# Both ends of the expert stage: weights signalled by kind, additions ahead of low parts, a down product between two halves of the last gate-up

## The chip, the cores and the metric

The kernel runs on one core of a Trainium2 chip. The metric is the time of one execution on the device in microseconds (us), lower is better. Engines are named as in the profile: PE is TensorE, PEld its weight loads, DVE is VectorE, ACT is ScalarE, POOL is GpSimd, SP is SyncE (it only issues DMAs here).

## What is computed

`x` is 8 sequences of 112 tokens of width 512, that is 896 tokens.

```python
x = x + attention(layernorm(x), ctx, Wq, Wkv_expand, Wout)     # 16 heads of 32, causal mask
h = layernorm(x)
scores = softmax(h @ gate_weight.T); topk_w, topk_idx = top_k(scores, 2)     # 8 experts
gu = einsum('th,efh->tef', h, gate_up_weights)                 # 512 -> 2 x 352 for each expert
y = einsum('tef,te,ehf->th', silu(gu[..., :F]) * gu[..., F:], combine, down_weights)
sgu = h @ shared_gate_up.T                                     # shared expert, 512 -> 2 x 704
y = y + (silu(sgu[:, :Fs]) * sgu[:, Fs:]) @ shared_down.T
out = x + y
```

## The kernel before

Each engine has an instruction stream of its own, written out by hand, and waits for the others by named semaphores. Products are made in fp32r from split operands: a value is held as a high part (rounded, written by a copy on ACT or POOL) and a low part (value less high part, written by DVE), and three products hi x lo, lo x hi, hi x hi stand for one.

Attention comes first, then the shared expert, six blocks of its inner width (`shared_gu`, `shared_down`; NJ = 6, ND = 5), whose results `add_shared` on DVE adds into `xres`. Meanwhile the tokens are sorted by expert and written by an indirect DMA into 21 tiles (NT) of 128 rows in DRAM; each tile belongs to one expert, whose number is read from `eid` by a `value_load` on every engine that addresses weights.

The expert stage runs over the 21 tiles. For tile i:

- SP loads it (`load_x`, semaphore `xin`); PE transposes it (`t_x`) into bank `S[2]`; ACT and DVE split it (`xs_hi`, `xs_lo`).
- ACT and DVE split the expert's gate-up weights in four chunks of 128 rows (`gu_hi`, `gu_lo`, buffer `gu_parts`), each as soon as the previous tile's product of the same chunk has been made.
- PE makes `gate_up(i)`: four chunks x three split passes x two banks (gate columns into `S[0]`, up columns into `S[1]`), 24 products. Each chunk counts one on `eg`.
- ACT takes silu of the gate bank, DVE multiplies it with the up bank (`expert_act`, semaphore `eact`).
- PE makes `down(i - 1)` (six split products and one plain one for the last 96 rows), then `t_act(i)`, the transposes of the activations, which ACT and DVE split again (`put_actT`, `aT_lo`).
- Two 128 x 512 high parts of the down weights are written by ACT (`dn_hi`) and POOL (`dn_hi1`), one low part for both by DVE (`dn_lo`).
- ACT copies y of tile i - 1, scaled by the routing weight, into `y_sb` (`put_y`, semaphore `ey`); POOL adds it into `out` with an indirect DMA (L505) after it has waited for the landing of the one before it (`yst`), since two rows of one token may not be added at once.

On PE tiles 2 to 19 are a loop (`Fori`); tiles 0, 1 and 20 are written out. The last tile is done without splits: `put_last_actT` and a DVE copy give `act_last`, and `last_down` makes its product in two column parts, which `put_last_y` copies out. `fill_with_transposes` makes transposes that nobody reads.

At the beginning of the stage PE has still to make the last shared product (`shared_down(ND - 1, ...)`): four banks of t = 0, then `t_x(0)`, then two of the three banks of t = 1, then `gate_up(0)`. The banks of t = 1 are those of t = 0, so each waits for an addition (`sres`). All expert weights are signalled on one semaphore, `we`, except the last three down weights, on `we_late`, whose loads are issued when the shared gate-up weights have been used. ACT waits for `we` before it splits the first gate-up chunk:

```python
act.wait_ge(s["pos"], 3)
act.wait_ge(s["we"], 16 * (3 * E - 2 * n_late))
act.wait_ge(s["sg"], NBLK * NJ)
e = expert(0)
for c in range(C):
    gu_hi(e, 0, c, first=True)
```

Here E = 8, C = 4, n_early = 1 and n_late = 3: eight gate-up loads, and two DMAs for each of the five early down weights.

Of the kernel before, what the change touches and what calls it, by code (L numbers as in the profile page):

```python
# [42 lines left out]
def build(nc, x, ctxT, wqT, wkvT, woT, gateT, guT, dnT, sguT, sdnT, out):  # L43
    NB, SQ, H = x.shape
    L = ctxT.shape[0]
    C = H // P
# [3 lines left out]
    E = guT.shape[0]  # L50
    F = dnT.shape[1]
# [9 lines left out]
    NX = T // P  # L61
# [162 lines left out]
    def ring_parts(b):  # L224
# [6 lines left out]

    names = (

        "x0 xt1 xt2 xrest wq0 wq1 wq2 wq3 wkeys wvals wo wgate ctx0 ctx1 wsg0 wsg1 wsd0 wsd1 wsd2 we we_late "

        "const zt sel zero wgpad sumg idf "

# [15 lines left out]
    with nc.Block() as block:  # L253
# [3 lines left out]
        def _(sp):  # L257
# [42 lines left out]
            def load_gu(e, sem):  # L300
                sp.dma_start(w_gu[:, e * GU:(e + 1) * GU], guT[e].rearrange("p c f -> p (c f)")).then_inc(sem, 16)

            def load_dn(e, sem):
                k2 = F // P * P
                at = w_dn[:, e * DN:(e + 1) * DN].rearrange("p (k d) -> p k d", d=H)
                sp.dma_start(at[:, 0:k2 // P, :],
                             dnT[e, 0:k2, :].rearrange("(k p) d -> p k d", p=P)).then_inc(sem, 16)
                sp.dma_start(at[0:F - k2, k2 // P, :], dnT[e, k2:F, :]).then_inc(sem, 16)
# [17 lines left out]
                sp.dma_start(xs_in[:, 0:H], xs_dram[bass.ds(i * P, P), 0:H]).then_inc(s["xin"], 16)  # L326

            for e in range(0, 2):
                load_gu(e, s["we"])
            next_sd(2)  # L330
            next_sg(2)
            for e in range(2, 5):
                load_gu(e, s["we"])
            next_sg(3)
            next_sd(3)
            for e in range(5, E):
                load_gu(e, s["we"])
            for e in range(n_early):
                load_dn(e, s["we"])
            next_sd(5)  # L340
            next_sg(4)
            next_sd(4)
# [4 lines left out]
            sp.wait_ge(s["ysum0"], 16)  # L347
            load_x(0)
            for e in range(n_early, E - n_late):
                load_dn(e, s["we"])  # L350
            sp.dma_start(dest[:, :, :], xs_dram[:, H:H + 2].bitcast(U32).rearrange("(n p) o -> p n o", p=P),
                         allow_slow_non_contiguous=True).then_inc(s["dest"], 16)
            sp.wait_ge(s["sg"], NBLK * NJ)
            for e in range(E - n_late, E):
                load_dn(e, s["we_late"])


            sp.wait_ge(s["Tx"], 1)
# [20 lines left out]
        def _(pool):  # L379
# [102 lines left out]
            scatter(1, "scat2")  # L482

            pool.wait_ge(s["pos"], 3)
            pool.wait_ge(s["we"], 16 * (3 * E - 2 * n_late))
            pool.wait_ge(s["we_late"], 16 * 2 * n_late)
            pool.wait_ge(s["sdn"], NX * ND)

            def dn_hi1(i):
                e = pool.value_load(eid[0:1, i:i + 1], min_val=0, max_val=E - 1)  # L490
                if i >= 1:
                    pool.wait_ge(s["edn_split"], i)
                pool.tensor_copy(dn2[0][:, 1, :], w_dn[:, bass.ds(e * DN + H, H)]).then_inc(s["dn_hi1"], 1)  # L493

# [16 lines left out]
        def _(pe):  # L511
# [316 lines left out]
            def gate_up(i, chunks=range(C)):  # L828

                pe.wait_ge(s["xs_hi"], i + 1)  # L830
                pe.wait_ge(s["xs_lo"], i + 1)
                for c in chunks:
                    pe.wait_ge(s["gu_hi"], C * i + c + 1)
                    pe.wait_ge(s["gu_lo"], C * i + c + 1)
                    for n, (x_, w_) in enumerate(((0, 1), (0, 0), (1, 0))):
                        for dst, f0 in ((S[0], 0), (S[1], F)):
                            ins = pe.matmul(dst[:, 0:F], xsT[x_][:, c, :], gu2[w_][:, c, f0:f0 + F],  # L837
                                            start=c == 0 and n == 0, stop=c == C - 1 and n == 2)
                    ins.then_inc(s["eg"], 1)

            def expert(i):
                return pe.value_load(eid[0:1, bass.ds(i, 1)], min_val=0, max_val=E - 1)

            def down(i, e):
                pe.wait_ge(s["aT_hi"], i + 1)
                pe.wait_ge(s["aT_lo"], i + 1)
                pe.wait_ge(s["dn_hi"], i + 1)
                pe.wait_ge(s["dn_hi1"], i + 1)
                pe.wait_ge(s["dn_lo"], i + 1)
                product(A[:, :], [(both(actT_split, every, k, every), both(dn2, every, k, every)) for k in range(2)],  # L850
                        stop=False).then_inc(s["edn_split"], 1)
                pe.wait_ge(s["aT"], i + 1)
                w = FK[2][1]
                pe.matmul(A[:, :], actT_plain[0:w, :], w_dn[0:w, bass.ds(e * DN + 2 * H, H)],  # L854
                          start=False, stop=True).then_inc(s["edn"], 1)
# [17 lines left out]
            def t_act(i):  # L873
                pe.wait_ge(s["eact"], i + 1)
                for k, (f0, w) in enumerate(FK):
                    ins = pe.transpose((S[3] if k < 2 else B)[0:w, k * P:(k + 1) * P], act_e[:, f0:f0 + w], ident[:, :])  # L876
                ins.then_inc(s["Ta"], 1)
# [6 lines left out]
            gate_up(1)  # L884
            t_x(2)
            pe.wait_ge(s["pos"], 3)
            pe.wait_ge(s["we"], 16 * (3 * E - 2 * n_late))
            pe.wait_ge(s["we_late"], 16 * 2 * n_late)
            down(0, expert(0))
            t_act(1)  # L890
            with pe.Fori(2, NT - 1) as i:
# [4 lines left out]
                down(i - 1, e)  # L896
                t_act(i)
            e_last = [expert(i) for i in (NT - 2, NT - 1)]
            gate_up(NT - 1)
            pe.wait_ge(s["ey"], NT - 2)  # L900
            down(NT - 2, e_last[0])
            t_act(NT - 1)
            fill_with_transposes(S[2], 5)
            pe.wait_ge(s["sres"], NX * ND)
            last_down(NT - 1, e_last[1])

# [2 lines left out]
        def _(act):  # L909
# [195 lines left out]
                hi(dn2[0][:, 0, :], w_dn[:, bass.ds(e * DN, H)], "dn_hi")  # L1105

            def silu(i):
                act.wait_ge(s["eg"], C * (i + 1))
                act.activation(silu_e[:, :], S[0][:, 0:F], ACT.Silu).then_inc(s["esil"], 1)  # L1109

            def put_y(i):
# [23 lines left out]
                act.activation(actT_plain[0:w, :], B[0:w, 2 * P:3 * P], ACT.Copy).then_inc(s["aT"], 1)  # L1135

            act.wait_ge(s["pos"], 3)
            act.wait_ge(s["we"], 16 * (3 * E - 2 * n_late))

            act.wait_ge(s["sg"], NBLK * NJ)  # L1140
            e = expert(0)
# [3 lines left out]
            for i in range(NT):  # L1145
                if i + 1 < NT:
                    e_next = expert(i + 1)
                    for c in range(C - 1):
                        gu_hi(e_next, i + 1, c)
                if i == NT - 1:  # L1150
                    silu(i)
                    put_last_actT(i)
                    put_y(i - 1)
                    break
                silu(i)
                xs_hi(i + 1)
                gu_hi(e_next, i + 1, C - 1)
                if i == 0:
                    act.wait_ge(s["sdn"], NX * ND)
                    act.wait_ge(s["we_late"], 16 * 2 * n_late)  # L1160
                    act.wait_ge(s["dest"], 16)
                dn_hi(e, i)
                if i >= 1:
                    put_y(i - 1)
                put_actT(i)
                e = e_next
# [4 lines left out]
        def _(dve):  # L1171
# [324 lines left out]

            def expert_act(i):
                dve.wait_ge(s["esil"], i + 1)
                dve.tensor_tensor(act_e[:, :], S[1][:, 0:F], silu_e[:, :], ALU.mult).then_inc(s["eact"], 1)  # L1499

            def aT_lo(i):
# [3 lines left out]
            for c in range(C):  # L1505
                if c == 2:
                    xs_lo(0)
                gu_lo(e, 0, c)
                add_shared(ND - 1, 0, c, c + 1)
            add_shared(ND - 1, 1, 0, 2)  # L1510
            for i in range(NT):
                if i + 1 < NT:
# [51 lines left out]
```

## Time and profile before

| | |
|---|---|
| median of 3 runs | 351.46 us (351.35 to 352.0) |
| profiled execution | 353.07 us, its span 351.3 us |
| PE busy | 332.9 us (95% of the span) |
| DVE, ACT, POOL busy | 271.6, 230.0, 118.5 us |
| mean granted clock of PE | 0.992 of 2.4 GHz |

Times in the rows are us from the start of the span; a duration is that of one instruction or of a merged group (x24: 24 of them). "[0.51 <-DVE xres]" is idle time of the engine just before, and who ended it. A matmul's own duration overlaps with that of the next; in the chain only the part that nothing else covers is counted.

### The profile page before, as it was taken

Reading aid. Unit: us, or ns where it says so; the run is one execution under the profiler, and the core shown is the slowest. Engines: PE = TensorE matmul, PEld = TensorE weight load, DVE = VectorE, ACT = ScalarE, POOL = GpSimd, SP = SyncE. Lnnn points to the kernel's source line nnn. Section 1 sums busy time; section 2 is a strip of 40 time slices with the busy share of each in tenths; the row PEclk is TensorE's granted clock in tenths of the full one; section 3 lists DMA queues with packets and bytes.
Section 4 is the critical chain, followed back from the end, with each engine's and each line's share of the span. In section 5 each row is a group of like instructions: output and inputs, shape, how many; then the busy total and the mean of one; then the engine's idle time right before and its main releaser. Section 6 shows DMA issues by size and latency. Waiting matters only on the chain.

```text
span 351.3 us, 7091 instructions
## 1 busy us (share of the span) xinstructions
PE 332.9 (95%) x2281; PEld 280.5 (80%) x2282; DVE 271.6 (77%) x464; ACT 230.0 (65%) x586; POOL 118.5 (34%) x136
## 2 busy tenths in 40 slices
PE   6999989999999999999999999999999999999980
PEld 6898877777776797988897878898889889988860
DVE  4798978999946258835586998999899899989900
ACT  3577899999973233213235578888888888888720
POOL 3332753555541000256200033343244234324411
PEclk9999999999999999999999999999999999999996
DMA  7999100000003799993599735434443543444233
GB/s 253 368 349 380 64 3 2 3 2 2 2 2 108 284 331 387 400 355 129 169 292 246 261 101 86 93 60 72 82 88 60 82 92 67 67 82 91 30 41 49
DMA packets 29051, 49.47 MB, mean 141 GB/s; under 512 B 7136, under 2 KB 12256, under 8 KB 28000
## 3 DMA queue, kind: packets, MB, share of 16 engines
q1 hardware_dynamic: 24880, 39.91, 35.0%
q0 software_dynamic: 4144, 9.23, 15.0%
q8 instruction: 13, 0.21, 0.3%
q14 instruction: 14, 0.11, 0.1%
HBM read 32.22 MB, written 16.92 MB: 140 GB/s over the span
## 4 chain that ended last, share of the span: by engine, by line
PE 54%; ACT 14%; DVE 10%; DMA 9%; issue 5%; POOL 4%; SPq 1%; POOLq 1%; ACTq 0%; DVEq 0%
PE bank L837 22%; PE bank L524 19%; ACT prob L956 8%; PE bank L854 5%; POOL xs_dram L474 4%; DMA xs_dram<-x2n,slot_i 3%; DMA w_dn<-dnT 3%; PE bank L708 2%; PE bank L876 2%; ACT probT L911 2%; PE bank L737 1%; DMA out<-y_sb,dest 1%; DVE xres L1391 1%; DMA w_sg<-sguT 1%; DMA ctx<-ctxT 1%
## 5 line engine op out<-in xcount | busy, mean ns | idle before, releaser
L1186 DVE TENSOR_TENSOR gu_parts<-w_gu,gu_parts 128x704 fp32r<-128x704 f32 x84 | 78.9, 972 | 1.7 <-ACT gu_parts L911 1.6
L911 ACT ACTIVATE gu_parts<-w_gu 128x704 fp32r x84 | 66.2, 794 | 18.4 <-PE bank L837 17.2
L837 PE MATMUL bank<-gu_parts,xsT_hi 128*128 128x352 f32 x336 | 69.5, 328 | 0.8 <-DVE xsT_lo L1186 0.8
L837 PEld LDWEIGHTS bank<-gu_parts,xsT_hi 128*128 128x128 f32 x336 | 55.6, 189 | 1.6 <-issue 1.2
L493 POOL CAST dn_hi<-w_dn 128x512 fp32r x20 | 19.7, 984 | 101.0 <-PE bank L524 69.0
L505 POOL DMA_INDIRECT out<-y_sb,dest x21 | 33.3, 1585 | 22.9 <-ACT y_sb L1116 17.2
L837 PE MATMUL bank<-gu_parts,xsT_lo 128*128 128x352 f32 x168 | 40.9, 325 | 0.0
L524 PE MATMUL bank<-x2T_hi,w_sg_lo 128*128 128x512 f32 (+1 forms) x88 | 32.6, 371 | 0.3
L524 PE MATMUL bank<-x2T_hi,w_sg_hi 128*128 128x512 f32 (+1 forms) x88 | 32.0, 363 | 0.0
L524 PE MATMUL bank<-x2T_lo,w_sg_hi 128*128 128x512 f32 (+1 forms) x88 | 31.9, 363 | 0.0
L837 PEld LDWEIGHTS bank<-gu_parts,xsT_lo 128*128 128x128 f32 x168 | 29.3, 189 | 0.0
L911 ACT ACTIVATE act_s_hi<-act_s 128x512 fp32r<-128x512 f32 (+1 forms) x10 | 5.8, 578 | 32.4 <-DVE act_s L1371 20.2
L474 POOL DMA_INDIRECT xs_dram<-x2n,slot_i x14 | 14.3, 1019 | 37.1 <-DVE eid L1471 33.1
L1186 DVE TENSOR_TENSOR dn_lo<-w_dn,dn_hi 128x1024 fp32r<-128x1024 f32 x20 | 24.6, 1228 | 0.8 <-POOL dn_hi L493 0.8
L956 ACT ACTIVATE prob<-score,negmax 112x112 f32<-112x112 f32 x64 | 24.1, 411 | 0.0
L956 ACT ACTIVATE prob<-bank,negmax 112x112 f32<-112x112 f32 x64 | 21.8, 363 | 1.9 <-DVE negmax L1231 1.9
L1391 DVE TENSOR_TENSOR xres<-xres,bank 128x512 f32<-128x512 f32 x35 | 22.0, 677 | 0.0
L854 PE MATMUL bank<-w_dn,actT_plain 96*128 x40 | 20.5, 592 | 0.0
L524 PEld LDWEIGHTS bank<-x2T_hi,w_sg_lo 128*128 128x128 f32 x88 | 16.5, 188 | 4.9 <-issue 2.5
L1499 DVE TENSOR_TENSOR act_e<-bank,silu_e 128x352 f32<-128x352 f32 x21 | 11.0, 523 | 11.8 <-ACT silu_e L1109 11.8
L911 ACT ACTIVATE probT<-bank 112x448 f32<-112x448 f32 x32 | 16.6, 554 | 3.9 <-PE bank L708 3.9
L404 POOL TENSOR_TENSOR prob<-prob,rrow 112x448 f32<-112x448 f32 x16 | 14.7, 931 | 11.7 <-DVE rrow L1235 11.7
(196 smaller groups left out, 804.9 us busy)
## 6 DMA issues: line engine op xcount, KB each, us to landing
w_gu<-guT SPq DMA_DIRECT2D x8, 1408.0 KB, 9.7
xs_dram<-no_row SPq DMA_DIRECT2D x1, 5460.0 KB, 19.2
xs_in<-xs_dram SPq DMA_DIRECT2D x21, 256.0 KB, 2.6
w_dn<-dnT SPq DMA_DIRECT2D x8, 512.0 KB, 6.2
w_sg<-sguT SPq DMA_DIRECT2D x10, 256.0 KB, 5.6
w_dn<-dnT SPq DMA_DIRECT2D x8, 192.0 KB, 6.7
w_sd<-sdnT SPq DMA_DIRECT2D x5, 256.0 KB, 4.8
out<-xres SPq DMA_DIRECT2D x1, 1280.0 KB, 5.4
```

Source lines behind the costliest of these rows:

```text
L404: pool.tensor_tensor(prob[r][:, :, :], prob[r][:, :, :], rrow[:, r, :].unsqueeze(2).to_broadcast([SQ, C, SQ]), ALU.mult)\
L474: pool.indirect_dma_start(out=xs_dram[:, :], out_offset=bass.IndirectOffsetOnAxis(ap=slot_i[:, k, n:n + 1], axis=0), in_=x2n[:, n, :], in_ ...
L493: pool.tensor_copy(dn2[0][:, 1, :], w_dn[:, bass.ds(e * DN + H, H)]).then_inc(s["dn_hi1"], 1)
L505: pool.indirect_dma_start(out=out[:, :], out_offset=bass.IndirectOffsetOnAxis(ap=dest[:, i, 0:1], axis=0), in_=y_sb[i % 2][:, :], in_offse ...
L524: ins = pe.matmul(dst, a, b, start=start and n == 0, stop=stop and n == len(passes) - 1)
L837: ins = pe.matmul(dst[:, 0:F], xsT[x_][:, c, :], gu2[w_][:, c, f0:f0 + F], start=c == 0 and n == 0, stop=c == C - 1 and n == 2)
L854: pe.matmul(A[:, :], actT_plain[0:w, :], w_dn[0:w, bass.ds(e * DN + 2 * H, H)], start=False, stop=True).then_inc(s["edn"], 1)
L911: act.activation(dst, src, ACT.Copy).then_inc(s[sem], 1)
L956: ins = act.activation(prob[r][:, c, :], src, ACT.Exp, bias=negmax[:, r, c:c + 1], accum_out=rowsum[:, r, c:c + 1])
L1186: dve.tensor_tensor(lo_, src, hi_.bitcast(F32), ALU.subtract).then_inc(s[sem], 1)
L1391: dve.tensor_tensor(xres[:, n, :], xres[:, n, :], (B, CC, D, A)[i][:, :], ALU.add)\
L1499: dve.tensor_tensor(act_e[:, :], S[1][:, 0:F], silu_e[:, :], ALU.mult).then_inc(s["eact"], 1)
```

## The change

1. The semaphore `we` becomes `wegu` (eight gate-up loads) and `wedn` (early down weights); `we_late` is now `wedn_late`. ACT waits for `wegu` ahead of its first chunk and for `wedn` ahead of its first `dn_hi`. POOL makes its first `value_load` ahead of its waits for down weights and shared products.
2. DVE makes each of the first four `add_shared` ahead of `gu_lo` of the same chunk, not behind it.
3. The last gate-up is made in two halves: chunks 0 and 1 in the usual order, then `down(19)`, then chunks 2 and 3, all gate columns first (`last_gate_then_up`). Silu of tile 20 waits for the gate columns only, the product on DVE for both.
4. ACT copies y of tile 19 ahead of silu(20). Fillers are eight ahead of `t_act(20)` (none before) and four behind it (five before).

```diff
-            for e in range(n_early):
-                load_dn(e, s["we"])
+            for e in range(n_early):
+                load_dn(e, s["wedn"])
...
             pool.wait_ge(s["pos"], 3)
-            pool.wait_ge(s["we"], 16 * (3 * E - 2 * n_late))
-            pool.wait_ge(s["we_late"], 16 * 2 * n_late)
-            pool.wait_ge(s["sdn"], NX * ND)

             def dn_hi1(i):
                 e = pool.value_load(eid[0:1, i:i + 1], min_val=0, max_val=E - 1)
-                if i >= 1:
+                if i == 0:
+                    pool.wait_ge(s["wedn"], 16 * 2 * (E - n_late))
+                    pool.wait_ge(s["wedn_late"], 16 * 2 * n_late)
+                    pool.wait_ge(s["sdn"], NX * ND)
+                else:
                     pool.wait_ge(s["edn_split"], i)
...
+            def last_gate_then_up(chunks):
+                i = NT - 1
+                for dst, f0 in ((S[0], 0), (S[1], F)):
+                    for c in chunks:
+                        pe.wait_ge(s["gu_hi"], C * i + c + 1)
+                        pe.wait_ge(s["gu_lo"], C * i + c + 1)
+                        for n, (x_, w_) in enumerate(((0, 1), (0, 0), (1, 0))):
+                            ins = pe.matmul(dst[:, 0:F], xsT[x_][:, c, :], gu2[w_][:, c, f0:f0 + F],
+                                            start=False, stop=c == C - 1 and n == 2)
+                    ins.then_inc(s["eg"], 1)
...
-            gate_up(NT - 1)
+            gate_up(NT - 1, range(C // 2))
             pe.wait_ge(s["ey"], NT - 2)
             down(NT - 2, e_last[0])
+            last_gate_then_up(range(C // 2, C))
+            fill_with_transposes(S[2], 8)
             t_act(NT - 1)
-            fill_with_transposes(S[2], 5)
+            fill_with_transposes(S[2], 4)
...
-                act.wait_ge(s["eg"], C * (i + 1))
+                act.wait_ge(s["eg"], C * (i + 1) - (i == NT - 1))
...
-            act.wait_ge(s["we"], 16 * (3 * E - 2 * n_late))
+            act.wait_ge(s["wegu"], 16 * E)
...
                 if i == NT - 1:
+                    put_y(i - 1)
                     silu(i)
                     put_last_actT(i)
-                    put_y(i - 1)
                     break
...
                 if i == 0:
                     act.wait_ge(s["sdn"], NX * ND)
-                    act.wait_ge(s["we_late"], 16 * 2 * n_late)
+                    act.wait_ge(s["wedn"], 16 * 2 * (E - n_late))
+                    act.wait_ge(s["wedn_late"], 16 * 2 * n_late)
...
                 dve.wait_ge(s["esil"], i + 1)
+                if i == NT - 1:
+                    dve.wait_ge(s["eg"], C * NT)
...
+                add_shared(ND - 1, 0, c, c + 1)
                 gu_lo(e, 0, c)
-                add_shared(ND - 1, 0, c, c + 1)
```

## Rows read from the trace of the kernel before

**Rows 1.** The page: granted clock of PE in 40 slices of 8.8 us, tenths.

```profile
PEclk9999999999999999999999999999999999999996
```

**Rows 2.** The chain, a gate-up in the loop: start, us, what.

```profile
317.70 3.89 PE bank L837 x24
```

**Rows 3.** The chain at the beginning of the stage: the load ACT waits for.

```profile
178.32 9.49 DMA w_dn<-dnT
```

**Rows 4.** Timeline of PE there: start, us, instruction, idle time ahead and its releaser.

```profile
187.03 0.40 PE L524 MATMUL bank<-w_sd_hi,act_s_lo 128*128 128x512 f32 x1
...
188.19 0.39 PE L524 MATMUL bank<-w_sd_hi,act_s_lo 128*128 128x512 f32 x1
...
190.47 0.46 PE L737 MATMUL bank<-ident_f,xs_in 128*128 128x128 f32 x4
191.44 0.47 PE L524 MATMUL bank<-w_sd_hi,act_s_lo 128*128 128x512 f32 x1 [0.51 <-DVE xres L1391]
...
194.00 0.81 PE L837 MATMUL bank<-gu_parts,xsT_hi 128*128 128x352 f32 x4
```

**Rows 5.** Timeline of ACT and DVE there.

```profile
186.97 0.53 ACT L911 ACTIVATE act_p<-silu_s 64x384 fp32r<-64x384 f32 x1 [0.74 <-DVE silu_s L1371]
...
187.53 0.55 DVE L1380 TENSOR_TENSOR act_p<-silu_s,act_p 64x384 fp32r<-64x384 f32 x1 [0.59 <-ACT act_p L911]
...
188.74 2.83 ACT L911 ACTIVATE gu_parts<-w_gu 128x704 fp32r x4 [1.25 <-DMA w_dn<-dnT]
...
189.68 0.89 DVE L1186 TENSOR_TENSOR gu_parts<-w_gu,gu_parts 128x704 fp32r<-128x704 f32 x1 [1.60 <-ACT gu_parts L911]
```

**Rows 6.** Timeline of POOL, DVE and PE where PE enters its loop.

```profile
201.59 0.61 POOL L493 CAST dn_hi<-w_dn 128x512 fp32r x1 [32.00 <-issue]
...
202.35 1.23 DVE L1186 TENSOR_TENSOR dn_lo<-w_dn,dn_hi 128x1024 fp32r<-128x1024 f32 x1 [0.83 <-POOL dn_hi L493]
...
206.59 0.55 PE L876 MATMUL bank<-ident,act_e 128*128 128x128 f32 x3
207.91 0.89 PE L837 MATMUL bank<-gu_parts,xsT_hi 128*128 128x352 f32 x4 [0.77 <-DVE xsT_lo L1186]
```

**Rows 7.** The chain at the end.

```profile
331.38 4.03 PE bank L837 x24
...
337.64 0.34 PE bank L876 x3
...
338.29 0.69 ACT y_sb L1116
...
339.24 4.93 DMA out<-y_sb,dest
```

**Rows 8.** Timeline of all engines at the end.

```profile
332.06 1.56 POOL L505 DMA_INDIRECT out<-y_sb,dest  x1 [0.64 <-ACT y_sb L1116]
...
333.23 0.41 DVE L1186 TENSOR_TENSOR actT_split_lo<-bank,actT_split_hi 128x256 fp32r<-128x256 f32 x1
...
335.94 0.52 DVE L1499 TENSOR_TENSOR act_e<-bank,silu_e 128x352 f32<-128x352 f32 x1 [2.30 <-ACT silu_e L1109]
...
338.56 2.87 PE L865 MATMUL bank<-w_dn,act_last 96*128 x12
...
340.86 0.98 ACT L1123 ACTIVATE y_sb<-bank,dest 128x384 f32<-128x384 f32 x2 [1.89 <-PE bank L865]
344.92 1.54 POOL L505 DMA_INDIRECT out<-y_sb,dest  x1 [4.13 <-DMA out<-y_sb,dest]
```

**Rows 9.** Tile w_gu from 130 us: the last loads of gate-up weights, issue times.

```profile
L301 SPq DMA_DIRECT2D w_gu<-guT x3: 431/432/433, 136.1 to 137.0; - x3
```

**Rows 10.** DMA issues from 190 to 192 us: KB, us from issue to landing.

```profile
xs_in<-xs_dram SPq DMA_DIRECT2D x1, 256.0 KB, 5.8
```

**Rows 11.** Timeline of DVE in the loop, pairs of low parts.

```profile
326.73 1.70 DVE L1186 TENSOR_TENSOR gu_parts<-w_gu,gu_parts 128x704 fp32r<-128x704 f32 x2
...
330.06 2.10 DVE L1186 TENSOR_TENSOR gu_parts<-w_gu,gu_parts 128x704 fp32r<-128x704 f32 x2
```

More of the change, by code:

```diff
@@ L232, in build @@
     names = (
-        "x0 xt1 xt2 xrest wq0 wq1 wq2 wq3 wkeys wvals wo wgate ctx0 ctx1 wsg0 wsg1 wsd0 wsd1 wsd2 we we_late "
+        "x0 xt1 xt2 xrest wq0 wq1 wq2 wq3 wkeys wvals wo wgate ctx0 ctx1 wsg0 wsg1 wsd0 wsd1 wsd2 wegu wedn wedn_late "
         "const zt sel zero wgpad sumg idf "
@@ L328, in _ @@
             for e in range(0, 2):
-                load_gu(e, s["we"])
+                load_gu(e, s["wegu"])
             next_sd(2)
@@ L332, in _ @@
             for e in range(2, 5):
-                load_gu(e, s["we"])
+                load_gu(e, s["wegu"])
             next_sg(3)
@@ L336, in _ @@
             for e in range(5, E):
-                load_gu(e, s["we"])
+                load_gu(e, s["wegu"])
             for e in range(n_early):
-                load_dn(e, s["we"])
+                load_dn(e, s["wedn"])
             next_sd(5)
@@ L349, in _ @@
             for e in range(n_early, E - n_late):
-                load_dn(e, s["we"])
+                load_dn(e, s["wedn"])
             sp.dma_start(dest[:, :, :], xs_dram[:, H:H + 2].bitcast(U32).rearrange("(n p) o -> p n o", p=P),
@@ L354, in _ @@
             for e in range(E - n_late, E):
-                load_dn(e, s["we_late"])
+                load_dn(e, s["wedn_late"])
             sp.wait_ge(s["Tx"], 1)
@@ L886, in _ @@
             pe.wait_ge(s["pos"], 3)
-            pe.wait_ge(s["we"], 16 * (3 * E - 2 * n_late))
-            pe.wait_ge(s["we_late"], 16 * 2 * n_late)
+            pe.wait_ge(s["wedn"], 16 * 2 * (E - n_late))
+            pe.wait_ge(s["wedn_late"], 16 * 2 * n_late)
             down(0, expert(0))
```

## Prediction

> **What bounds the kernel now.** I read the page first: TensorE is busy 95% of the span and its granted clock is high in every slice but the last [rows 1], so time can only be won where TensorE waits or where the end hangs on something else. Then the chain that ended last, over the expert stage. From tile 3 to tile 19 it is TensorE alone: the gate-ups of tiles 18 and 20 start at 317.70 and 331.38, two tiles of 6.84 us [rows 2, 7], the same for every tile between. Reordering can win nothing there, and the change touches nothing there. At both ends the chain leaves TensorE, and those are the places to price.
>
> At the beginning the chain runs over a down weight that lands at 187.82 [rows 3], ScalarE's first gu_parts at 188.74 after 1.25 idle, VectorE's low part at 189.68 after 1.60 idle [rows 5], an addition of the shared result behind it, and TensorE, which waits 0.51 for that addition till 191.44 [rows 4]. All this time the result to be added was there: the next bank's products start at 187.03 [rows 4], so the first bank was full near 187.2.
>
> A second place is the loop's entry [rows 6]: VectorE stands 0.83 idle for GpSimd's first cast at 201.59, then works without a gap of note up to xsT_lo of tile 2, and 0.77 after that TensorE starts gate-up(2), at 207.91. Its activation transposes had ended at 206.59 + 0.55 = 207.14.
>
> At the end [rows 7, 8] gate-up(20) ends at 331.38 + 4.03 = 335.41 and down(19) at 337.64, but y of tile 19 is copied out only at 338.29 to 338.98, since ScalarE does silu(20) and act_last first. Its scatter goes at 339.24 (0.27 after the copy), takes 4.93, lands at 344.17, and 0.75 later, at 344.92, the last scatter starts. The last y had been ready since 340.86 + 0.98 = 341.84. So the end hangs on the scatter of tile 19, and the last y has 344.92 - 341.84 - 0.27 = 2.8 us of slack.
>
> **The start, edit by edit.** ScalarE's wait for the gate-up weights only: the last of those loads was issued at 137.0 [rows 9], fifty us ahead, so it is passed at once. ScalarE's sequencer is then free when the act_p copy has gone out at 186.97 [rows 5]. From the landing to the first chunk it needed 188.74 - 187.82 = 0.92, value load and dispatch. The first chunk therefore starts near 187.9, 0.85 earlier; the four (2.83) end at 190.7, when the transposes of x (190.47 and about 0.3) have just ended. xsT_hi follows at once, and xsT_lo is ready near 192.1.
>
> Additions in front of the low parts are the same instructions, swapped. VectorE's own value load can follow 187.53 [rows 5], so the first addition goes at 187.53 + 0.92 = 188.45 and ends at 189.1; the second, behind a low part of 0.8, ends at 190.6. TensorE wants them at 190.76 and 191.92, five products of one tile taking 187.03 to 188.19 = 1.16 [rows 4]. Both waits are gone: gate-up(0) starts at 190.76 + 2 x 1.16 = 193.08, not 194.00. Its own needs are there (xsT_lo 192.1, two low parts 191.4); chunks 2 and 3, now behind additions, come at 193.6 and 195.0 and are wanted a half and three quarters through, at 195.0 and 196.0. Gain 0.92.
>
> What is late next is x of tile 1: issued when the transposes of tile 0 are done, about 190.96, it took 5.8 [rows 10] and lands at 196.8, and that does not move. TensorE will want it after gate-up(0), at 193.08 + 3.89 = 196.97. It just fits. The down weights' waits now stand on ScalarE ahead of its first dn_hi, eleven us after the first chunk, with y and the activation split behind; even loads as slow as the 9.49 of [rows 3], issued by 189.7, would be in by 199.2, about when it comes there. I cost it at nothing.
>
> GpSimd's waits behind the value load: the last shared product ended near 199.5 and the cast came at 201.59, 2.1 later, of which I take the value load to be most. With it done beforehand the cast comes near 198.7 and VectorE's 0.83 goes. But the cast then lies beside a low part: a pair of low parts that shares its time with a cast takes 2.10, a pair without 1.70 [rows 11]. I charge 0.40. VectorE's chain to xsT_lo(2) moves by 0.9 + 0.83 - 0.4 = 1.33 and gate-up(2) with it, to 206.58. TensorE itself would be ready at 207.14 - 0.92 = 206.22. So the bounds of the start are 0.9 (the cast brings nothing) and 1.7. I take **1.3**.
>
> The Trainium skill (SBUF — State Buffer, Who interferes with whom) says that a VectorE instruction with two SBUF inputs and a GpSimd one that reads SBUF exclude each other, the later being blocked for the whole of the other. By it the cast could cost VectorE its full 0.61, and the time would be 0.2 above my forecast. The trace agrees that they contend, with 0.40.
>
> **The end, edit by edit** (times as in the trace of before, the start's gain not taken off). Gate-up(20) starts at 331.38; half of it is done at 333.4. Down(19) now comes here and needs actT_split_lo, which VectorE ends at 333.64 [rows 8]. This is the new wait: TensorE goes on at 333.75. Down takes 2.23 as before (335.41 to 337.64) and 0.1 to restart, and ends at 336.1. y(19) is now first on ScalarE, 336.12 to 336.81, and its scatter goes at 337.08, if scatter 18 is in; that went at 332.06, and with 19's 4.93 and the 0.75 it would allow 337.74. It was 339.24.
>
> Behind put_y on ScalarE stand silu(20) and act_last. Of the second half, gate columns end at 336.1 + 0.97 = 337.07, when ScalarE is free, up columns at 338.05. Silu and product took 335.41 to 336.46 [rows 8], hidden under down(19); now silu is hidden by the up columns and the product's 0.52 is exposed, till 338.6, where VectorE's added wait for both halves holds nothing else up. The eight fillers lie over it. Three transposes take 0.34 [rows 7], 0.11 each, so eight end at 338.93, 0.3 after the data: the fill, not the data, sets it. Then t_act until 339.27. From its end to last_down it was 338.56 - 337.98 = 0.58 with five fillers, so with four 0.47: last_down at 339.75. From there to the last y it is 341.84 - 338.56 = 3.28, giving 343.05, and its scatter can go at 343.32.
>
> Scatter 19 lands at 337.08 + 4.93 = 342.0 and allows the last at 342.75. The last y is the later, so the last scatter starts at 343.3 instead of 344.92; from there to the end nothing changes. Gain **1.6**. Bounds: 2.2 if only the scatters count; 0.8 if an issue stall as long as TensorE's 0.77 of [rows 6] stands in the rewritten tail.
>
> The Trainium skill (DMA: Bandwidth & Descriptors, Anatomy of one DMA — SWDGE (gpsimd) path) gives about 2.0 us plus bytes / 436e3. An estimate by it for 256 KB is 2.6 us; by that the old end would have hung on scatter 19 only until 342.6, and a last y at 343.05 would lose some 0.7 at this end. The trace shows 4.93 for this scatter and decides against it.
>
> **The sum.** 1.3 + 1.6 = 2.9 us. The profiled execution took 353.07 (span 351.3, 1.8 around it), so 350.2 for one like it. The median of the runs, 351.46, lies 1.6 below the profiled one; with the same difference, 348.5.
>
> **Rivals.**
> - Start lost: x of tile 1 comes late, or VectorE's chain does not shorten. For it stands that x has 0.2 us to spare, against it 2.4 us of idle time on VectorE. 0.3 + 1.6: 349.6.
> - End half lost: a stall of 0.8 in the tail. For it: the half product waits on VectorE's last instruction and new code is fetched; against: leaving the loop cost 0.14 (4.03 for 3.89). 1.3 + 0.8: 349.4.
> - More: TensorE enters the loop when it is ready, and the last y does not hold up. 1.7 + 2.2: 347.6.
> - The change doesn't do what it says: the value loads, not the waits, took the time, and another landing replaces 19's. 351.4.
> - Slower: the 0.35 gap ahead of down(19), with little work around it, lets the clock fall from 2.4 to 1.2 GHz. Left from there are 2.3 + 1.9 + 0.9 + 0.3 + 2.9 = 8.3 us of TensorE, doubled; 8.3 - 2.9 = 5.4 lost: 356.9. It decides as soon as 2.9 us of work is doubled. Against it: the gap of 0.77 at 207 left the clock's slice at 9, and only the last slice, which holds no product, reads 6 [rows 1].
>
> **How the numbers follow.** Forecast 0.53 (its own range 347.9 to 349.2), start lost 0.13, end half lost 0.12, more 0.10, nothing 0.05, slower 0.07. The first four, 0.88, lie in 347.4 to 350.1, which takes in the bounds of both ends. A measurement of this kernel can tell about 0.2%, 0.7 us: faster 0.88, same 0.05, slower 0.07.
>
> **What would show it.** Start: ScalarE's first gu_parts near 187.9, no wait of TensorE at 191, gate-up(0) at 193.1, the cast near 198.7, gate-up(2) near 206.6. End, counted from the start of gate-up(20): down(19) at +2.4 (was +4.0), its scatter at +5.7 (was +7.9), the last at +11.9 (was +13.5), released by y and not by a landing. I am wrong if the last scatter is still released by a landing beyond +13, if x of tile 1 shows as a wait, or if the granted clock drops ahead of the last product.

## The result and the profile after

Seven runs of each kernel on one chip: 351.39 us before (350.69 to 352.25), 349.79 us after (349.05 to 351.91). The ratio is 0.9949, 95% interval 0.9925 to 0.9973: 1.8 us faster, between 0.9 and 2.6; the two medians lie 1.6 apart. The forecast was 348.5, 2.9 us faster, in a range of 347.4 to 350.1. The time lies in that range, near its slow end and outside the 347.9 to 349.2 that I had given the forecast itself. The gain came out at some two thirds of what I had summed up, and 2.9 lies just outside the interval.

The profiled execution after took 349.05 us with a span of 347.3, 4.0 less than the one before. That is more than the change gives. The first product with `act_p` (L767 before, L768 after), which closes the first bank of the last shared product and which no edit reaches, starts at 186.49 before and at 185.37 after, so 1.1 us is not of the change. I therefore count from this product, called R below, up to the loop, and from the start of gate-up(20) at the end. These are timeline starts; the chain of [rows 7] has gate-up(20) at 331.38, since it counts only what nothing else covers. Timeline of TensorE in the kernel before: R, gate-up(1), gate-up(20) and down(19):

```profile
186.49 0.47 PE L767 MATMUL bank<-w_sd_lo,act_p 128*128 128x512 f32 x1
...
200.02 0.88 PE L837 MATMUL bank<-gu_parts,xsT_hi 128*128 128x352 f32 x4
...
331.30 0.88 PE L837 MATMUL bank<-gu_parts,xsT_hi 128*128 128x352 f32 x4
...
335.25 0.40 PE L524 MATMUL bank<-dn_hi,actT_split_lo 128*128 128x512 f32 x1
```

The start, TensorE's timeline in the kernel after (start, us, instruction, idle time ahead), against [rows 4, 6]:

```profile
185.37 0.47 PE L768 MATMUL bank<-w_sd_lo,act_p 128*128 128x512 f32 x1
...
189.35 0.46 PE L738 MATMUL bank<-ident_f,xs_in 128*128 128x128 f32 x4
189.65 0.46 PE L525 MATMUL bank<-w_sd_hi,act_s_lo 128*128 128x512 f32 x1
...
191.99 0.80 PE L838 MATMUL bank<-gu_parts,xsT_hi 128*128 128x352 f32 x4
...
197.90 0.89 PE L838 MATMUL bank<-gu_parts,xsT_hi 128*128 128x352 f32 x4
...
205.26 0.88 PE L838 MATMUL bank<-gu_parts,xsT_hi 128*128 128x352 f32 x4 [0.30 <-issue]
```

The wait of 0.51 behind the transposes of x is gone. Gate-up(0), (1), (2) start at 6.62, 12.53 and 19.89 from R; before it was 7.51, 13.53 and 21.42. ScalarE, GpSimd and VectorE there, against [rows 5, 6]:

```profile
185.85 0.53 ACT L925 ACTIVATE act_p<-silu_s 64x384 fp32r<-64x384 f32 x1 [0.74 <-DVE silu_s L1386]
186.78 2.84 ACT L925 ACTIVATE gu_parts<-w_gu 128x704 fp32r x4 [0.41 <-issue]
...
197.72 2.10 DVE L1201 TENSOR_TENSOR gu_parts<-w_gu,gu_parts 128x704 fp32r<-128x704 f32 x2
197.75 1.32 POOL L494 CAST dn_hi<-w_dn 128x512 fp32r x1 [29.29 <-PE bank L769]
199.74 1.21 DVE L1201 TENSOR_TENSOR dn_lo<-w_dn,dn_hi 128x1024 fp32r<-128x1024 f32 x1
```

The first chunk comes 0.93 after the copy of act_p goes out, with no landing in its way, and dn_lo follows without a wait. The cast now lies beside a pair of low parts, which takes 2.10, as in the loop [rows 11].

The end, all engines, against [rows 7, 8]:

```profile
328.71 0.88 PE L838 MATMUL bank<-gu_parts,xsT_hi 128*128 128x352 f32 x4
...
331.22 0.47 PE L525 MATMUL bank<-dn_hi,actT_split_lo 128*128 128x512 f32 x1 [0.34 <-issue]
...
333.74 0.69 ACT L1130 ACTIVATE y_sb<-bank,dest 128x512 f32<-128x512 f32 x1 [4.17 <-PE bank L866]
334.70 0.46 ACT L1123 ACTIVATE silu_e<-bank 128x352 f32<-128x352 f32 x1 [0.27 <-PE bank L849]
334.85 1.55 POOL L506 DMA_INDIRECT out<-y_sb,dest  x1 [3.86 <-ACT y_sb L1130]
335.45 1.03 PE L883 MATMUL bank<-ident 128*128 128x128 f32 x8
335.72 0.52 DVE L1516 TENSOR_TENSOR act_e<-bank,silu_e 128x352 f32<-128x352 f32 x1 [4.71 <-PE bank L849]
336.32 0.52 PE L888 MATMUL bank<-ident,act_e 128*128 128x128 f32 x3
...
337.44 2.87 PE L877 MATMUL bank<-w_dn,act_last 96*128 x12 [0.15 <-issue]
339.74 0.98 ACT L1137 ACTIVATE y_sb<-bank,dest 128x384 f32<-128x384 f32 x2 [2.47 <-PE bank L877]
340.99 1.54 POOL L506 DMA_INDIRECT out<-y_sb,dest  x1 [4.59 <-ACT y_sb L1137]
```

What released the last scatter was a landing before, [4.13 <-DMA out<-y_sb,dest] in [rows 8]; now it is y. From gate-up(20)'s start: down(19) at 2.51 (3.95 before), its scatter at 6.14 (7.94), last y ready at 12.01 (10.54), last scatter at 12.28 (13.62). The last y is 1.5 us later and the last scatter 1.3 us earlier. In these two traces the start won 21.42 - 19.89 = 1.53 and the end 1.34; with the 1.12 ahead of R that is all of the 4.0 between the spans.

### The profile page after: what moved, and what is told of

Read it like the earlier page. It is cut to its first block, busy times and chain, and to the rows that moved or that the text cites. A ratio compares the mean times of both kernels' runs of the same rounds, so it can differ in the third digit from the quotient of the medians.

```text
span 347.3 us, 7108 instructions
## 1 busy us (share of the span) xinstructions
PE 333.8 (96%) x2288; PEld 282.7 (81%) x2289; DVE 271.9 (78%) x464; ACT 230.3 (66%) x586; POOL 120.1 (35%) x136
## 4 chain that ended last, share of the span: by engine, by line
PE 74%; ACT 13%; DVE 6%; issue 3%; DMA 2%; POOLq 1%; POOL 1%; SPq 0%; DVEq 0%
PE bank L525 35%; PE bank L838 23%; ACT prob L970 8%; PE bank L866 5%; PE bank L888 2%; PE bank L709 2%; PE bank L738 2%; ACT probT L925 2%; PE bank L609 2%; DMA out<-y_sb,dest 1%; DVE xnT_lo L1201 1%; DMA w_sg<-sguT 1%; DVE prob L1254 1%; PE bank L517 1%; PE bank L580 1%
## 5 line engine op out<-in xcount | busy, mean ns | idle before, releaser
L838 PE MATMUL bank<-gu_parts,xsT_hi 128*128 128x352 f32 x328 | 67.9, 328 | 0.3 <-issue 0.3
L838 PEld LDWEIGHTS bank<-gu_parts,xsT_hi 128*128 128x128 f32 x328 | 54.2, 189 | 1.2 <-issue 1.0
L494 POOL CAST dn_hi<-w_dn 128x512 fp32r x20 | 20.7, 1035 | 97.8 <-PE bank L525 68.5
L838 PE MATMUL bank<-gu_parts,xsT_lo 128*128 128x352 f32 x164 | 39.9, 324 | 0.0
L866 PE MATMUL bank<-w_dn,actT_plain 96*128 x40 | 20.5, 591 | 0.0
```

## The experiments

Twelve runs, ten of altered kernels and one each of the two kernels once more. The traces of all are summed up first, in us: gate-up(0) to (2) and ScalarE's first chunk from R; TensorE's wait for x of tile 1; last y ready and last scatter from gate-up(20)'s start. "Landing" means that ScalarE's first chunk waited for a down weight to land, "free" that it did not.

| kernel | ACT chunk | gu(0) | gu(1) | gu(2) | x wait | last y | last scatter |
|---|---|---|---|---|---|---|---|
| before | 2.25, landing | 7.51 | 13.53 | 21.42 | 0 | 10.54 | 13.62 |
| before_again | 2.83, landing | 8.10 | 14.11 | 22.04 | 0 | 10.54 | 13.33 |
| y_first | 3.31, landing | 8.57 | 14.59 | 22.27 | 0 | 13.90 | 14.17 |
| end_only | 1.46, free | 6.73 | 12.75 | 20.75 | 0 | 12.05 | 12.32 |
| start_only | 1.41, free | 6.62 | 13.51 | 20.96 | 0.93 | 10.54 | 13.38 |
| after | 1.41, free | 6.62 | 12.53 | 19.89 | 0 | 12.01 | 12.28 |
| after_again | 1.41, free | 6.62 | 13.74 | 21.19 | 1.17 | 12.01 | 12.28 |
| fill0 | 1.42, free | 6.62 | 12.53 | 19.89 | 0 | 12.02 | 12.29 |
| gate_first_undone | 1.41, free | 6.62 | 12.53 | 19.88 | 0 | 12.45 | 12.72 |
| x_ahead_of_one | 1.41, free | 6.61 | 12.52 | 20.00 | 0 | 12.00 | 12.27 |
| dest_behind_x | 1.41, free | 6.62 | 12.87 | 23.99 | 0.29 | 12.03 | 12.31 |
| pool_undone | 1.41, free | 6.63 | 12.53 | 20.44 | 0 | 12.04 | 12.31 |
| adds_undone | 1.41, free | 6.70 | 13.23 | 20.62 | 0.50 | 12.01 | 12.28 |
| actwait_undone | 2.79, landing | 6.94 | 14.71 | 22.10 | 1.73 | 12.02 | 12.30 |

The four top ones have the old start, the others the new one, whole, less one part, or with its loads in another order.

**after_again**: the changed kernel, unaltered.

> The changed kernel, unaltered, once more. Theory A (both ends won 1.5 and 1.3 us, as the first trace of it shows, and the rest is chance): the stretch between the start of the last shared down product of half t = 0 and gate-up(2), 20.83 us now and 22.36 before, and the stretch from gate-up(20) to the last scatter, 12.24 now and 13.54 before, come out the same within 0.2 us; the ratio to before is about 0.992 (2.8 us). Rival B (something outside the two ends gives part of it back in most executions): the two stretches repeat, but the ratio stays at 0.995, and the part ahead of the expert stage is longer than in the trace of before.

349.9 us to 352.27 of the kernel before on the same chip, ratio 0.9944 (0.992 to 0.9967). The first result repeats; the interval rules out neither 0.992 at its edge nor 0.995. The end repeats to 0.01 us. The start does not: gate-up(0) is where it was, but then TensorE waits.

```profile
197.42 0.53 PE L738 MATMUL bank<-ident_f,xs_in 128*128 128x128 f32 x4 [1.17 <-DMA xs_in<-xs_dram]
```

x of tile 1 landed 1.2 us too late, and gate-up(2) came at 21.19, close to the 21.42 of the kernel before. This is the first rival of the prediction, in some executions and not in others. Theory A's "within 0.2" fell for the start. Rival B has the ratio right, but not its cause: what was given back lies in the start itself.

**start_only** and **end_only**: one half of the change each.

```diff
# start_only: the changed kernel with the end of the kernel before
-            gate_up(NT - 1, range(C // 2))
+            gate_up(NT - 1)
...
-            last_gate_then_up(range(C // 2, C))
-            fill_with_transposes(S[2], 8)
...
# end_only: the changed kernel with the three edits of the start undone
+            act.wait_ge(s["wedn"], 16 * 2 * (E - n_late))
...
-                add_shared(ND - 1, 0, c, c + 1)
                 gu_lo(e, 0, c)
+                add_shared(ND - 1, 0, c, c + 1)
```

> Only parts 1 and 2 of the change (signals by kind, POOL's value load ahead of its waits, additions in front); the end as before. Theory A: from the last shared down product of t = 0 to gate-up(2) it takes 20.8 us instead of 22.4; gate-up(20) to the last scatter stays at 13.5; ratio 0.9956 (1.5 us). Rival (the start's gain is taken back later by the loop): the beginning of the loop comes earlier but gate-up(20) does not, ratio 1.0.

> Only parts 3 and 4 of the change (down(19) between the halves, gate columns first, y of tile 19 first, fillers 8 and 4); the start as before. Theory A: gate-up(20) to the last scatter takes 12.2 us instead of 13.5, ratio 0.9963 (1.3 us). Rival (scatters set the end whatever the order, and the last landing only slides): the last scatter is released by a landing again and the stretch takes over 13.0, ratio 0.999 to 1.

Ratios 0.9981 (0.9958 to 1.0005) and 0.9989 (0.9965 to 1.0014). Theory A had said 0.9956 and 0.9963, and each lies just outside its interval; 1.0, no change, lies inside both. So the runs show neither half by itself, and added up they give 1.1 us where both together gave 1.8 and 2.0. Medians on that chip: 352.27 before, 351.67, 351.28, and 349.9 with both. Times of single executions spread over 3 us and more, so the traces must tell. In end_only's trace the last scatter is at 12.32, released by y: the end does its work alone, and the rival of a sliding landing falls. In start_only gate-up(0) is at 6.62, but x of tile 1 was 0.93 late, so gate-up(2) was 20.96 and not 19.9.

**fill0**: no transposes ahead of the last `t_act`.

```diff
-            fill_with_transposes(S[2], 8)
```

> The changed kernel without the eight fillers ahead of the last activation transposes. Theory A (the fillers, not the data, set the start of these transposes, as worked out beforehand): in the trace of after the data are there at 336.24 and the fillers end at about 336.49, so the transposes come 0.2 us earlier and the last scatter 0.2 earlier, at 12.05 from gate-up(20). Rival (they hold the clock up): the granted clock falls ahead of the last product and last_down, 2.87 us, takes more than 3.5 us.

Ratio 0.9959 (0.9935 to 0.9982). Last scatter at 12.29: nothing won, and last_down still takes 2.87. Both theories fell. act_e is ready 7.53 after gate-up(20)'s start in the kernel after (336.24 - 328.71) and 7.55 here (336.28 - 328.73), and the transposes start at 7.61 or 7.60 in either: the eight fillers end just as the data comes, and so cost nothing.

**x_ahead_of_one** and **dest_behind_x**: two ways to have x of tile 1 sooner.

```diff
# x_ahead_of_one
-            for e in range(E - n_late, E):
+            for e in range(E - n_late, E - 1):
                 load_dn(e, s["wedn_late"])
...
             load_x(1)
+            load_dn(E - 1, s["wedn_late"])
```

> The changed kernel with the load of the last down weight (704 KB) issued behind the load of x of tile 1 and not ahead of it. Theory A (in some executions x of tile 1 lands after gate-up(0), behind the late down weights, and holds TensorE): no wait of TensorE for xs_in; from the first act_p product (the reference point, first L768 row of the stage) to gate-up(1) it takes 12.5 us and to gate-up(2) 19.9, as in the first trace of the changed kernel and unlike the 13.7 and 21.2 of its second; median 0.5 to 1 us under that of the changed kernel. Rival B (x was late by chance of that one execution and costs little in the mean): median as the changed kernel. Rival C (the displaced weight is now what is late): a wait of ScalarE or GpSimd for a landing of w_dn ahead of dn_hi, reference point to gate-up(2) over 20.5.

> The changed kernel with the table of destinations (21 KB in elements of 8 bytes, over 2,600 packets) loaded behind x of tile 1. Theory A: the table occupies the DMA engines for about 2 us, in which 5 to 20 GB/s move, so x of tile 1 lands up to 2 us earlier and TensorE does not wait for it; gate-up(1) at 12.5 and gate-up(2) at 19.9 from the reference point. Rival C: the table itself is now late, ScalarE waits for it ahead of its first dn_hi and gate-up(2) comes at over 20.5. Rival B: nothing measurable.

x_ahead_of_one: 349.86 us to 352.14 before, ratio 0.9939 (0.9915 to 0.9964). Its trace has no wait for x although it was in the worse position: its stage loads (x of tile 0, the down weights right behind) began 11.4 us ahead of R, as in after_again (11.3), and not 13.3 as in the first trace of the changed kernel. That fits theory A, but in time it can't be told from the changed kernel (0.9949, 0.9944), so B's "costs little in the mean" isn't ruled out either. dest_behind_x has 0.9927 (0.99 to 0.9954); its profiled execution took 354.04 us and is not in that ratio. In it x of tile 1 is late by 0.29 and x of tile 2 by 1.34, so the wait moved one tile on. Most of what makes gate-up(2) so late there, 23.99, comes behind that wait: TensorE idles once more, for 0.99, and then its granted clock falls to 0.50, its level of 1.2 GHz, and the products of down(0) follow each other at 0.43 us and not 0.23. TensorE's timeline, and a window with busy times and, as the number behind POOL's, the granted clock:

```profile
204.42 0.53 PE L738 MATMUL bank<-ident_f,xs_in 128*128 128x128 f32 x4 [1.34 <-DMA xs_in<-xs_dram]
205.95 0.77 PE L525 MATMUL bank<-dn_hi,actT_split_lo 128*128 128x512 f32 x1 [0.99 <-issue]
206.51 0.63 PE L525 MATMUL bank<-dn_lo,actT_split_hi 128*128 128x512 f32 x1
```

```profile
206.00:208.00 2.00, 2.00 (x5) 1.61 (x6) 1.92 (x3) 0.27 (x1) 0.00 (x0) 0.50 0.47 131
```

How the table of destinations holds the DMA engines is seen in after_again; the view of DMA from 185 to 189 us, first line busy tenths in 40 slices, second GB/s:

```profile
DMA  9999999999999999688754433320359992249924
GB/s 369 328 309 288 189 92 156 115 137 97 98 97 77 96 93 51 9 9 8 6 6 5 5 5 3 2 3 21 102 123 246 307 184 82 82 143 184 123 82 143
DMA packets 2935, 0.45 MB, mean 112 GB/s; under 512 B 2727, under 2 KB 2727, under 8 KB 2935
```

In 4 us 2,727 packets under 512 bytes, and the engines busy while they move under 160 GB/s and then under 10. That the loads of down weights, and x of tile 1 behind them, are late by this is not shown: with the table moved behind it, x of tile 1 still took 6.4 us from issue to landing, against 5.8 in [rows 10]. Theory A of dest_behind_x fell in that trace; gate-up(2) passes rival C's 20.5, but by the wait for x and by the clock, since ScalarE's first dn_hi waits for nothing.

**pool_undone** and **adds_undone**: one edit of the start taken back.

```diff
# pool_undone
+            pool.wait_ge(s["wedn"], 16 * 2 * (E - n_late))
+            pool.wait_ge(s["wedn_late"], 16 * 2 * n_late)
+            pool.wait_ge(s["sdn"], NX * ND)
...
-                if i == 0:
...
+                if i >= 1:
```

> The changed kernel with GpSimd's waits ahead of its first value load again. Theory A (the value load, about 2 us, was on VectorE's way to the loop): the first cast comes 2.1 us after the last shared product and not at 0.4, VectorE idles for it, and gate-up(1) to gate-up(2) takes 7.9 us instead of 7.4. Rival (TensorE's own entry into the loop sets it): 7.4 as with it.

> The changed kernel with the four additions behind the low parts again. Theory A (once ScalarE is early, the order is worth little, since the first addition only has to be done when TensorE comes to the bank again): gate-up(0) at 6.7 us from the reference point instead of 6.6. Rival, as I worked it out beforehand (both edits together win 0.9 and the first addition at 190.6 was what held TensorE): with low parts first, the addition ends behind TensorE's arrival and gate-up(0) comes at 7.0 or later.

pool_undone, 0.9978 (0.9958 to 0.9998): gate-up(1) to (2) takes 7.91, where it is 7.36 with the edit and 7.89 before. VectorE waits for the cast again:

```profile
200.34 0.62 POOL L493 CAST dn_hi<-w_dn 128x512 fp32r x1 [31.43 <-issue]
...
201.09 1.22 DVE L1200 TENSOR_TENSOR dn_lo<-w_dn,dn_hi 128x1024 fp32r<-128x1024 f32 x1 [0.85 <-POOL dn_hi L493]
```

Theory A holds: the value load ahead of its waits is worth 0.55 us at the loop's entry. adds_undone, 0.9962 (0.9941 to 0.9983): gate-up(0) at 6.70, so with ScalarE early the order of additions is worth 0.08. Theory A again; its rival, my own reasoning, fell.

**actwait_undone** and **before_again**: what the landing of a down weight costs.

```diff
# actwait_undone
             act.wait_ge(s["wegu"], 16 * E)
+            act.wait_ge(s["wedn"], 16 * 2 * (E - n_late))
```

> The changed kernel, but ScalarE waits for the early down weights too ahead of its first chunk. Theory A: where they land by the time ScalarE comes there, gate-up(0) stays at 6.6 us from the reference point; where they land later, each us late shows in full, up to 7.5. Rival (the order of additions alone covers the wait): 6.6 with ScalarE's chunk released by the landing.

> The kernel before, unaltered, once more. It should come out at 1.000. What I want is a second trace of the old start. Theory A (the old start was held by the landing of a down weight in some executions only): reference point (first act_p product) to gate-up(0) is either 7.5 us, with ScalarE's first gu_parts released by the landing, or 6.7, with it free; to gate-up(2) 20.7 to 21.4; the new start's 19.9 to 21.2 overlaps with that. Rival B (the old start is the same each time): 7.5 and 21.4 again. Gate-up(20) to the last scatter: 13.4 to 13.6 in both.

before_again has 0.9991 (0.9974 to 1.0008). actwait_undone 0.993 (0.9907 to 0.9953) on six runs: in time it is not worse than the changed kernel. In its trace ScalarE waited 1.79 for the landing, and its first chunk came at 2.79 from R:

```profile
188.41 2.84 ACT L925 ACTIVATE gu_parts<-w_gu 128x704 fp32r x4 [1.79 <-DMA w_dn<-dnT]
...
192.56 0.87 PE L838 MATMUL bank<-gu_parts,xsT_hi 128*128 128x352 f32 x4 [0.16 <-issue]
...
198.33 0.54 PE L738 MATMUL bank<-ident_f,xs_in 128*128 128x128 f32 x4 [1.73 <-DMA xs_in<-xs_dram]
```

Yet gate-up(0) is at 6.94, only 0.32 late. With the old order of additions the same lateness, 2.83 in before_again, gave 8.10. In the three old starts that a landing held, gate-up(0) is 5.26 or 5.27 behind ScalarE's first chunk (7.51 - 2.25, 8.10 - 2.83, 8.57 - 3.31); here 4.15. "Each us late shows in full" fell. The two edits are two remedies for one stall: either alone leaves 0.08 to 0.32 us of it. And theory A of before_again holds in kind for the old start, which a landing held in three traces of four and left free in end_only. Its figures were too narrow: gate-up(0) came at 8.10 and 8.57 too, and gate-up(2) lies between 20.75 and 22.27.

**y_first**: the kernel before, with y of tile 19 first on ScalarE and nothing else.

```diff
                 if i == NT - 1:
+                    put_y(i - 1)
                     silu(i)
                     put_last_actT(i)
-                    put_y(i - 1)
```

> The kernel before, with one edit only: ScalarE copies y of tile 19 ahead of silu(20). Theory A (the old end hangs on scatter 19, the last y has 2.8 us of slack): scatter 19 goes 0.6 us earlier, 7.3 from gate-up(20) instead of 7.9; the last y comes later, about 12.1 instead of 10.5, as silu, product and transposes are pushed back by the copy, and the last scatter at about 12.9 instead of 13.5, still released by the landing. Rival (the last y decides as soon as it is pushed back): the last scatter is released by y and at 13.3 or later.

Ratio 1.0004 (0.9978 to 1.0031): nothing won. Scatter 19 went at 7.35 as worked out, but the last y came at 13.90 and not 12.1. TensorE's timeline, and two windows as above:

```profile
336.69 1.02 PE L854 MATMUL bank<-w_dn,actT_plain 96*128 x2
339.41 0.55 PE L876 MATMUL bank<-ident,act_e 128*128 128x128 f32 x3 [1.69 <-DVE act_e L1499]
339.79 0.97 PE L871 MATMUL bank<-ident 128*128 128x128 f32 x5
340.55 4.31 PE L865 MATMUL bank<-w_dn,act_last 96*128 x12
```

```profile
340.00:342.00 2.00, 2.00 (x8) 1.21 (x7) 0.28 (x1) 0.37 (x1) 0.27 (x1) 0.52 0.63 68
342.00:344.00 2.00, 2.00 (x5) 1.16 (x4) 0.00 (x0) 0.00 (x0) 0.00 (x0) 0.62 0.36 64
```

TensorE stood 1.69 us without a product; about 0.7 us after it had started again, at 340.1, the granted clock fell to 0.50, its level of 1.2 GHz, and it was back at 1.00 near 343.5. last_down took 4.31 for 2.87. With the 0.26 of the slower fillers that is 1.7 us, just what the last y is late (13.90 - 1.7 = 12.2). The rival here was right in that y decides, by a mechanism it didn't name. One trace alone shows the fall, and it may not come in every execution: of the ten runs three, the profiled one among them, have a mean granted clock of 0.988 or 0.989 and took 353.49 to 353.67 us; the other seven have 0.993 or 0.994 and a median of 351.6. What the reordering gives where the clock stays up is open.

**gate_first_undone**: the second half in the usual order.

```diff
-            last_gate_then_up(range(C // 2, C))
+            gate_up(NT - 1, range(C // 2, C))
...
-                act.wait_ge(s["eg"], C * (i + 1) - (i == NT - 1))
+                act.wait_ge(s["eg"], C * (i + 1))
```

> The changed kernel with the second half of the last gate-up in the usual order, silu waiting for all of it. Theory A (in the changed kernel the last y bounds): silu's 0.47 us is exposed, the last y comes at 12.4 instead of 12.0 from gate-up(20) and the last scatter at 12.7 instead of 12.3. Rival (the landing of scatter 19 bounds): scatter 19 goes at 6.2 as before, and the last at 12.3, unmoved.

Ratio 0.9961 (0.993 to 0.9991). Scatter 19 at 6.04, last y at 12.45, last scatter at 12.72, 0.44 later: the last y bounds in the changed kernel, and gate columns first are worth 0.44 us.

## Why the prediction was right, and where it was off

**The start, first chunk and gate-up(0).** Right to 0.03 us: 187.9 and 193.08 counted from R are 1.41 and 6.59, measured 1.41 and 6.62. But the 0.92 is no constant. It was made against one trace of before; in the old starts gate-up(0) was at 7.51, 8.10, 8.57 and 6.73, so the gain there is 0.1 to 1.9, by when the early down weights land.

**The two edits summed as one.** I gave both waits to the two edits together, which was right, and didn't ask what either does alone. Each alone does nearly all (0.08 and 0.32 us left, in one trace each).

**GpSimd's value load.** Right. The cast at 12.38 from R (12.2 forecast) and 0.55 us at the loop's entry (0.83 - 0.40 = 0.43 forecast). The lone cast's neighbour cost 0.40 as charged: 2.10 for 1.70.

**x of tile 1.** "It just fits" was the weak step. It fitted in the first trace and in four others with the new start, and was late by 0.93, 1.17, 0.50, 0.29 and 1.73 in the remaining five. It was never late in the four with the old start. In three of these TensorE comes for it only at 11.39 to 12.45 from R, and not at 10.4; before_again, where x landed at 10.67, would have missed 10.4. But in end_only TensorE comes at 10.62, and x was in at 9.87. What decides the landing stays open. In the eight traces with the new start, whole or less one part, and the loads as they were, the first down load is issued 12.7 to 13.8 us ahead of R in the four without a wait and 10.9 to 12.2 in the four with one; end_only, at 11.4 and in time, does not fit this. In the traces with the whole new start and the loads as they were (after, after_again, start_only, fill0, gate_first_undone) gate-up(2) is at 19.89, 21.19, 20.96, 19.89 and 19.88, mean 20.36; in the four with the old start 21.42, 22.04, 22.27 and 20.75, mean 21.62. So 1.3 us were won in the mean, with a standard error of 0.45. That this is the number forecast is luck: it is a larger gain, partly given back by a wait that I had put at nothing.

**The end.** The mechanism held at each point: down(19) at 2.5, scatter 19 no longer decides, the last y, 1.5 us later than before, does. The size was off: the old last scatter stands at 13.62, 13.33 and 13.38 in the three traces with the end unaltered, mean 13.44, the new one at 12.27 to 12.32 in nine, so 1.1 us for the 1.6 forecast. Of the missing 0.5, 0.2 is that I took the old end from its slowest trace. 0.3 is the last scatter at 12.28 from TensorE's first product instead of 343.32 - 331.30 = 12.02, and it has two halves. First, down(19) between the halves took 333.70 - 331.22 = 2.48, where I had charged 2.23 + 0.1, so act_e is ready at 7.53 and not at 338.6 - 331.30 = 7.3. The 0.3 that I charged for the fillers behind it doesn't exist (fill0); what stands in the sum as filler is mostly this, and the fillers end at 336.48 - 328.71 = 7.77 for the 7.63 forecast. Second, I took 0.11 off behind the last transposes for one filler fewer, and nothing came of it: from there to last_down it is 337.44 - 336.48 = 0.96 with four fillers, and was 338.56 - 337.64 = 0.92 with five, where I had 0.82.

**The sum.** 1.3 + 1.1 = 2.4 by the traces, 1.8 by the first runs with an interval of 0.9 to 2.6 (2.0 by after_again's): they agree within what either can tell. The term that was mis-sized is the end's 1.6. Whether the rest, 0.6, is chance or something that the traces don't have stays open. The measured 349.79 is nearer to the prices of two rivals, 349.6 for "start lost" and 349.4 for "end half lost", than to 348.5; a part of each came: x late in half of the traces of the new start, and 0.3 of a longer tail.

**The slower rival** was priced for a gap of 0.35 and did not come: the clock was granted in full, 1.00, over a gap of 0.34 in the changed kernel and of about 0.7 in fill0 (335.65 to 336.33). y_first shows that the mechanism was real one edit away: with 1.69 it took, in the traced execution, all that the edit had won. The changed kernel has half a gate-up between down(19) and the transposes, where y_first has that gap. I ranked it by its chance for this kernel, rightly, but didn't see that it says which part of the change can't be left out.

**Better than both.** x_ahead_of_one has 0.9939 and no wait for x. dest_behind_x and actwait_undone have lower ratios, 0.9927 and 0.993, but waits for x in their traces. The intervals of all three take in the changed kernel's 0.9949 and 0.9944, so no run tells any of them from it.

## What to carry to other kernels

Before summing up what a stage's start gains, look at which terms end at a DMA landing: such a term is a distribution, and one trace gives one draw of it, both for the wait removed and for the next load that the earlier engine will meet. Where an end is a chain of serial scatters, let the copy-out that feeds them go ahead of all else, but fill what that exposes with real products; the same reordering without them (y_first) gained nothing here. When two edits cure one stall, take each back alone before keeping both.

## What the runs showed of the hardware that I had not expected

The length of a single gap does not tell whether TensorE's clock falls. It fell after 1.69 us without a product in y_first, and in dest_behind_x after 1.34 and 0.99 with 0.53 us of transposes between. It stayed at 1.00 after 1.73 in actwait_undone, 1.58 at the start of y_first (189.66 to 191.70) and 1.17 in after_again. Each is one trace. The window of actwait_undone in which TensorE starts again after its 1.73:

```profile
198.00:200.00 2.00, 1.67 (x10) 1.40 (x11) 0.95 (x3) 1.10 (x2) 0.00 (x0) 1.00 1.03 376
```

TensorE has two paces in the loop at the same granted clock of 1.00. A gate-up of 24 products takes 3.89 us in one and 3.81 in the other, and a tile 6.84 or 6.75. Twelve of the fourteen traces run at the first from beginning to end ([rows 2] is one such gate-up); after_again changes to the second at tile 6 and gate_first_undone at tile 4, and both stay with it. The chain of after_again, tile 16:

```profile
302.05 3.81 PE bank L838 x24
305.85 0.29 PE bank L738 x4
306.14 1.46 PE bank L525 x6
```

Over 15 tiles that is 1.3 us, about as much as either half of the change, and it is in a kernel's spread, not in its code: the same kernel did both. What decides it I can't say. It is also why the span of one execution says little here: after_again lost 1.3 us at the start and ended with a span of 347.8, 0.5 over the first trace.
